# A vision tower on one core: patches on 128 partitions, softmax scaled in nine pieces, a split scatter, earlier patch weights and new orders

## What is computed

```python
p = img2patches(x, 16, 16)                       # 196 x 768
h = layernorm(layernorm(p) @ W + b)              # embedding, 196 x 192
# causal attention, 12 heads of 16, with relative positions
qkv = _layernorm(h) @ w_attn + b_attn
scores = q @ k.T + q @ rel.T ; scores[j > i] = -inf
y = softmax(scores) @ v
h = h + y @ w_proj + b_proj
# routed block
normed = _ln(_layernorm(h), g1, b1)
s = sigmoid(normed @ Wr + br)
idx = the 29 tokens with the lowest s            # 15% of 196
attn_out = full attention of the chosen tokens over all, @ Wo + bo
mix_out = (normed + s * pooled) @ Wm + bm
hh = h' + where(chosen, attn_out, mix_out)
h = h + hh + gelu(_ln(hh) @ W1 + bf1) @ W2 + bf2
```

## Time and profile before

| | us |
|---|---|
| median of 3 runs | 5560.41 |
| lowest and highest | 5558.65, 5562.08 |
| profiled execution, its own time | 5558.0 |
| span in its profile | 5556.2 |
| PE, DVE, ACT, POOL busy | 5185.8, 4301.6, 3799.2, 2762.3 |

### The profile page before, as it was taken

How to read it: one execution, slowest core, us unless ns; L and a number is a source line. 1 busy time by engine, 2 the same in 40 slices (tenths; PEclk the granted TensorE clock), 3 DMA queues, 4 the chain that set the end, 5 groups by cost and what they waited for, 6 DMA issues and landing times.

```text
span 5556.2 us, 146436 instructions
## 1 busy us (share of the span) xinstructions
PE 5185.8 (93%) x48224; PEld 4863.6 (88%) x48224; DVE 4301.6 (77%) x12888; ACT 3799.2 (68%) x12542; POOL 2762.3 (50%) x3415
## 2 busy tenths in 40 slices
PE   3899999999999999999999999999999999999998
PEld 3888889889888888888988888888898888888887
DVE  2787777777778777777777777877777777787776
ACT  1667767776776776777677677677767767767775
POOL 4454554555455455455445545545544554554552
PEclk8999999999999999999999999999999999999999
DMA  3222222222222222222222222222222222222220
GB/s 52 37 29 30 35 31 30 32 34 30 29 37 29 30 36 30 30 32 34 30 29 37 29 30 36 30 30 33 34 30 29 37 30 29 36 30 30 33 33 6
DMA packets 229237, 175.82 MB, mean 32 GB/s; under 512 B 28423, under 2 KB 228699, under 8 KB 229207
## 3 DMA queue, kind: packets, MB, share of 16 engines
q1 hardware_dynamic: 218913, 172.63, 23.5%
q10 hardware_dynamic: 9110, 1.84, 0.2%
q0 software_dynamic: 1184, 0.97, 0.1%
HBM read 156.11 MB, written 19.27 MB: 32 GB/s over the span
## 4 chain that ended last, share of the span: by engine, by line
PE 59%; ACT 14%; DVE 13%; issue 6%; DVEq 5%; ACTq 2%; POOL 1%; POOLq 0%
PE banks L636 8%; PE banks L646 8%; PE banks L695 7%; PE banks L628 6%; PE banks L684 5%; PE banks L924 5%; DVEq L1359 4%; PE banks L620 3%; ACT p L1540 3%; PE banks L820 3%; DVE a_row L1127 3%; ACT L1518 3%; PE banks L719 2%; ACT gstore L1525 2%; DVE qk_parts L1341 2%
## 5 line engine op out<-in xcount | busy, mean ns | idle before, releaser
L1540 ACT ACTIVATE p<-banks,negmax 98x98 f32<-98x98 f32 (+1 forms) x3072 | 1141.8, 381 | 208.8 <-DVE negmax L1172 166.6
L517 POOL TENSOR_TENSOR p<-p,rden 98x392 f32<-98x392 f32 (+1 forms) x768 | 895.9, 1188 | 778.4 <-DVE rden L1186 778.4
L695 PE MATMUL banks<-tokw,x_sb 128*98 128x193 f32 x4096 | 765.8, 340 | 16.0 <-DVEq L1114 16.0
L695 PEld LDWEIGHTS banks<-tokw,x_sb 128*98 128x98 f32 x4096 | 716.0, 254 | 16.9 <-DVEq L1114 16.1
L1172 DVE TENSOR_REDUCE negmax<-banks 98x2 f32<-98x392 f32 (+1 forms) x1152 | 625.7, 553 | 131.0 <-PE banks L684 126.7
L526 POOL TENSOR_TENSOR gstore<-gstore 96x784 f32<-96x784 f32 x128 | 236.4, 1847 | 894.5 <-ACT gstore L1525 894.5
L684 PE MATMUL banks<-kz,qk_parts 128*98 128x392 f32 x2304 | 647.4, 385 | 0.0
L1540 ACT ACTIVATION_READ_ACCUMULATOR p<-banks,negmax 98x1 f32 x3072 | 619.4, 202 | 0.0
L924 PE MATMUL banks<-w,gparts 128*98 128x192 f32 x4608 | 508.8, 260 | 0.0
L719 PE MATMUL banks<-ident,p 98*98 98x98 f32 x4608 | 495.8, 251 | 3.8 <-ACTq L1544 2.9
L636 PE MATMUL banks<-z3Ts,w_split 128*128 128x196 f32 x3840 | 490.3, 280 | 1.4 <-DVE z3Ts L1143 1.4
(11 more groups left out here) (293 smaller groups left out, 12777.9 us busy)
## 6 DMA issues: line engine op xcount, KB each, us to landing
x_sb<-in_x SPq DMA_DIRECT2D x384, 196.0 KB, 4.8
x_sb<-in_x SPq DMA_DIRECT2D x384, 189.0 KB, 7.7
out<-out_row SPq DMA_DIRECT2D x128, 147.0 KB
pT<-in_L_tok_W SPq DMA_DIRECT2D x6, 96.0 KB
pT<-in_L_ffn_W ACTq DMA_DIRECT2D x1, 576.0 KB
gstore<-in_L_ffn_W SPq DMA_DIRECT2D x1, 384.0 KB
...
```

The source lines that it names most:

```text
L517: last = gp.tensor_tensor(heads, heads, rden[:, g, t].unsqueeze(2).broadcast_to([HT, 4, w]), ALU.mult)
L695: last = mm(bank[b][0:HT, t * (D + 1):(t + 1) * (D + 1)], xf[:, a:a + (HT - 1) * PS + 1:PS], tokw[:, q], start=t == 0 and q == 0, stop=q = ...
L1540: sc.activation((p1 if t else p0)[0:HT, 4 * g + s], bank[b][0:HT, w * i:w * i + w], ACT.Exp, bias=negmax[:, g, t, s:s + 1], accum_out=den[ ...
```

## The change

Six things change.

1. **Patches.** `x_sb` now has eight bands of 16 partitions (`XROWS`): (channel, first pixel) pairs, each with six columns. Since 3 x 16 = 48 columns of pixels fill 8 x 6 slots, the last two columns of channel 2 are held by two bands and are copied by POOL from partitions 32 to 63 into 96 to 127; that copy gives `xlast_sb`, and the squares and the first patch matmul wait for it instead of for `x_in`. A token half needs six matmuls, an image 12; an image is loaded with eight DMAs instead of six.
2. **Nine pieces.** `inverse_sums(u)` and `normalised(u)` go by unit; PE waits for the unit that a block needs.
3. **Scatter.** `ao` and `selT` are float32r; `ao` has a high and a low part, and the scatter is two accumulated passes for each half. The bias fbo enters through a row of ones in `ctxT` instead of an addition on DVE.
4. **Patch weights.** Their loads are issued first, on SP and ACT; DVE scales them and PE sums them ahead of the other weights. POOL issues no loads. The first turn stands ahead of `steps`, and DVE clears p1 and pT after `w_ready`.
5. **POOL.** h2b is made ahead of the rstd of h1.
6. **Orders** on PE, DVE and ACT.

```diff
-QH = PS // 2
-KX = 2 * C * PS
+QX = 6
+KX = 128
+XROWS = ((0, 0, 0), (16, 1, 0), (32, 2, 0), (48, 2, 8), (64, 0, 6), (80, 1, 6), (96, 0, 12), (112, 1, 12))
...
-                def normalised(g):
-
-                    gp.wait_ge(sem["rden_sb"], after("rden_sb", n, g + 1))
-                    for t, part, w in ((0, p0, HT), (1, p1, T)):
-                        heads = part[0:HT, 4 * g:4 * g + 4]
-                        last = gp.tensor_tensor(
-                            heads, heads, rden[:, g, t].unsqueeze(2).broadcast_to([HT, 4, w]),
-                            ALU.mult)
-                    last.then_inc(sem["pnorm_sb"], 1)
+                def normalised(u):
+
+                    g, t, slots, w = s_unit(u)
+                    s0, sn = slots[0], len(slots)
+                    gp.wait_ge(sem["rden_sb"], after("rden_sb", n, u + 1))
+                    heads = (p1 if t else p0)[0:HT, 4 * g + s0:4 * g + s0 + sn]
+                    gp.tensor_tensor(
+                        heads, heads,
+                        rden[:, g, t, s0:s0 + sn].unsqueeze(2).broadcast_to([HT, sn, w]),
+                        ALU.mult).then_inc(sem["pnorm_sb"], 1)
+                if head:
+                    xv = x_sb[:].rearrange("p h (w q) -> p (h w) q", q=PS)
+                    gp.drain()
+                    gp.wait_ge(sem["x_in"], after("x_in", l))
+                    gp.tensor_tensor(xv[96:128, :, 4:6], xv[32:64, :, 6:8],
+                                     ones[32:64, 0:1].unsqueeze(1).broadcast_to([32, T, 2]),
+                                     ALU.mult)
+                    gp.drain().then_inc(sem["xlast_sb"], 1)
...
-                        pe.wait_ge(sem["x_in"], after("x_in", l))
+                        pe.wait_ge(sem["xlast_sb"], after("xlast_sb", l))
...
                     for t in range(2):
-                        last = mm(bank[5][0:HT, t * D:(t + 1) * D],
-                                  selT[:, HT * t:HT * t + HT], ao[:], start=True,
-                                  stop=True)
+                        for part in range(2):
+                            last = mm(bank[5][0:HT, t * D:(t + 1) * D],
+                                      selT[:, HT * t:HT * t + HT], ao[:, part],
+                                      start=part == 0, stop=part == 1)
...
-                    ve.tensor_tensor(ao[0:SELP], bank[4][0:SELP, 0:D], fbo[:],
-                                     ALU.add).then_inc(sem["ao_sb"], 1)
+                    ve.tensor_copy(ao[0:SELP, 0], bank[4][0:SELP, 0:D])
+                    ve.drain()
+                    ve.tensor_tensor(ao[0:SELP, 1], bank[4][0:SELP, 0:D],
+                                     ao[0:SELP, 0].bitcast(F32),
+                                     ALU.subtract).then_inc(sem["ao_sb"], 1)
...
                 def squares():
-                    sc.wait_ge(sem["x_in"], after("x_in", l))
+                    sc.wait_ge(sem["xlast_sb"], after("xlast_sb", l))
...
-            sc.wait_ge(one["p1_zeroed"], 1)
...
+            sc.wait_ge(one["w_ready"], 1)
+            step(-3, -2, -1, 0, True, False, False, False, False)
+            sc.wait_ge(one["p1_zeroed"], 1)
+            sc.wait_ge(one["stores_zeroed"], 1)
```

384 lines of the change are left out of this document (215 added, 169 removed).

## The result

The changed kernel takes 5405.07 us (median of four runs, 5403.64 to 5407.90) against 5560.49 us for the kernel before on the same chip. The ratio is 0.972, its 95% interval 0.9706 to 0.9735. The profiled execution took 5405.0 us with a span of 5403.3. The forecast of 5400 us was 0.1% off. That is better than its working deserved: two errors of 53 and 61 us, of opposite sign, lie in it, and it is luck that they cancel.

A forecast was written before the change was run, and what follows sets the result against it. PE, busy 93%, was taken as the bound, over 127 turns of 42.08 us. A 24.6 plus B 16.3 makes 40.9, 1.18 less: 150 us, with 8 at the start 158, so 5400 us; range 5250 to 5540.

The forecast's parts named there:

- A: PE's stretch of a turn from the transposes of a_row to the routed scores: 24.77 us before, forecast 24.6.
- Patches: Patch matmuls in A: four fewer an image at 0.356 us each, 1.42 us a turn saved.
- Scatter: Scatter on PE in A: four F32R passes at 0.36 us replace two fp32 matmuls at 0.65, saving 0.29 us.
- down(0) and attn_out behind the projection: PE order: first third of the down matmuls and attn_out move from Stretch B into A, adding 1.72 us there.
- The copy of two columns: POOL's copy of 32 x 392 elements before squares and first patch matmul: 0.87 us, hidden by 0.5 us.
- Rival 4: Column copy late by 0.5 us or more: turn 41.8, 5514 us; chance 0.10 shared with half of Rival 2.
- Nine pieces: Normalisation products on POOL: 0.66 us more work, less 0.8 for narrower squares, called neutral; no gain on PE.
- Stretch B: From the routed scores to the next transposes of a_row: 17.31 us before, chain 15.99 plus 0.3 blocking, forecast 16.3.
- Rival 2: POOL's pieces block DVE at y_row, gelu casts and z0: turn 42.5 us, 5603 us; chance 0.08 in full.
- Start: Before the loop: loads +11 us, to w_ready -12.5, after it -6.8; together -8, between -19 and +11.
- rival 3: Turn not shortened, removed PE work becomes wait at the projection: Stretch B 17.3, A 24.8, 5550 us; chance 0.04.
- rival 1: Stretch B's chain shorter than walked, DVE never blocked: 15.2, A 24.3, turn 39.5, 5220 us; chance 0.18.

## Why the prediction was right, point by point

**The bound.** Right. The turn is the unit, 127 of them carry 202 us of the change, and PE work was worth its length in A: 0.27 of 0.28 us for the scatter.

**Patches.** The term 1.42 measured 1.34 in PE time and 0.96 in the turn. The error is in counting it and the shrinking wait for v_sb as separate gains: the wait went from 0.76 to 0.29 (forecast 0.35), but these 0.29 exist only since the patches are shorter.

**Scatter.** Forecast 0.29, measured 0.27.

**down(0) and attn_out behind the projection.** +1.72 in A as PE time was about right (A: 24.33 for 24.6; of the 0.27 between them, 0.20 are what was allowed for out_row and z0, for which no wait shows). attn_out's new place was not tried by itself. What failed is the view of the place that they left. The prediction named a wait of over 1 us at the projection as a sign of a right forecast and gave it no price. It costs 0.65 us a turn and 38 falls of the clock, 61 us. Neither the sum nor a rival had the clock, since the kernel before shows no fall in its loop. Even with a price for one fall, no row told their number: it changes with an edit that leaves the wait alone (38 falls at 1.37 us, 17 at 1.36). B was the same with and without down(0) (16.14 and 16.16).

**The copy of two columns.** 0.88 us for 0.87, at 2036.79, so it ends at 2037.67, and no wait of PE for it in the loop. The embedding starts at 2038.04 with no idle time: 0.37 us of cover for the 0.5 forecast. Rival 4 did not occur.

**Nine pieces.** The step that failed, beside the missing clock. The prediction called them neutral: it read that no wait of PE before ends on POOL's products, and concluded that nothing was to be gained. But B's chain, which the next paragraph of the prediction walks, goes through those products; the time stood in the wait at its end. Undone, they cost 0.92 us a turn. The forecast of the turn survived because the chain of B was added up with the pieces in it.

**Stretch B.** Forecast 16.3, measured 16.16. Link by link: scores to max2 2.03 (2.05); the three pieces 2.73 (2.60), with 0.27 of it a wait for the ninth reciprocal; a_row 0.66 (0.66). The blocking was met where it was named (DVE, then POOL):

```profile
2018.02 1.70 DVE L1171 TENSOR_SCALAR y_row<-y_row,mv_y,rstd 98x192 f32<-98x192 f32 x2
...
2017.94 1.66 POOL L519 TENSOR_TENSOR p<-p,rden 98x392 f32<-98x392 f32 x2
2019.87 0.84 POOL L519 TENSOR_TENSOR p<-p,rden 98x392 f32<-98x392 f32 x1 [0.27 <-DVE rden L1232]
```

y_row's two halves wait for both pieces, 1.03 us, one gparts cast loses 0.15, z3 0.68 (hidden). On the chain that makes 0.27 + 0.15 = 0.42 us for the 0.3 allowed. Rival 2 was right about y_row and wrong about its price: most of the blocking lies beside POOL's own work, which the chain needs anyway. Of the two gparts casts only one was held, and not by rstd but by h2b (2022.98 to 2023.99).

**Start.** -8.5 us for -8, with all three terms off: the loads +8.3 (11), from there to w_ready about -8.7 (-12.5), from w_ready to the first keys about -8.1 (-6.8). The preparation ahead is worth some 4 us in all, where the forecast put 2.4 us of DVE and 8.2 us of PE off the path: it had no price for the slow clock that follows PE's idle time, 4.3 us. The loads moved by 8.3 us, between the two bounds of the prediction (0 and 30); which of the two sets them stays open, since no run changed the queues alone.

**Signs.** The patch matmuls number 3072 with a mean of 336 ns (before 340), PE's busy time falls by 201 us, 1.6 a turn for 1.7, and the two longest waits of a turn are the two named (0.75 for the routed softmax, forecast 1.0; 1.37 at the projection). a_row takes 0.33 us a half:

```profile
L723 PE MATMUL banks<-tokw,x_sb 128*98 128x193 f32 x3072 | 573.5, 336 | 15.5 <-POOLq L531 15.5
```

One sign of rival 2 was there as well, y_row's halves with a mean of 0.85 us, without the rival's time.

**Rivals 1 and 3.** The turn did shorten, which answers rival 3 (A 24.33 and B 16.16, not 24.8 and 17.3). It did so to 40.48 and not to rival 1's 39.5, whose B of 15.2 is not there either. The kernel with down(0) in its old place comes near rival 1's turn, 39.8, but through A (23.7), with B at 16.14.

**The sum.** Turn 40.48 for 40.9: 53 us better than forecast. Falls: 61 us worse. Together 5405 for 5400. The bound was right, and stretches A and B came out within 0.3 us of the forecast; that 0.1% was hit is luck.

Undone one by one, the parts come to 0.96 + 0.92 + 0.52 + 0.27 - 0.65 = 2.02 us a turn, and the change brought 1.59. They need not add up, since three of them (the pieces, h2b and down(0)) act on the wait ahead of the projection; what the remaining orders do by themselves was not tried, apart from the keys.
